# A gated cross-attention and mixture-of-experts block: row stacks built by selection matmuls, one list of steps, experts per sequence

## The reference, cut to what matters

```
x = x + tanh(g_xattn) * attention(layernorm(x), ctx)                 # 256 x 512 scores per sequence, one head
X = layernorm(x)
q, k, v = rmsnorm(X, n1) @ wq, @ wk, @ wv                            # 16 heads of 8 features
X = X + softmax(q k^T / sqrt(8)) v @ wo                              # 256 x 256 scores, 64 (sequence, head) pairs
h2 = rmsnorm(X, n2)
combine = top-2 of softmax(h2 @ router)                              # 8 experts
X = X + shared_expert(h2) + sum_e combine[e] * expert_e(h2)          # silu(h2 @ gate) * (h2 @ up) @ down, 256 hidden
x = x + tanh(g_ffn) * X
```

## Time and profile before

| | us |
|---|---|
| median of 3 runs | 249.63 (249.5 to 251.0) |
| the profiled execution's own time | 249.14 |
| its span in the profile | 247.4 |
| mean granted PE clock | 0.92 of full speed |
| DMA | 12.83 MB, 50 GB/s of HBM traffic over the span |

### The profile page before, as it was taken

One profiled execution on the slowest core, in us unless ns is written; L12 is line 12 of the kernel. 1 busy time (PEld: TensorE's weight loads), 2 busy tenths in 40 slices (PEclk: granted clock), 3 DMA queues, 4 the chain that ended last, 5 costly groups with the idle time before them and its releaser, 6 DMA issues.

```text
span 247.4 us, 3838 instructions
## 1 busy us (share of the span) xinstructions
PE 202.7 (82%) x1327; PEld 161.2 (65%) x1327; DVE 152.5 (62%) x393; ACT 101.3 (41%) x203; POOL 58.8 (24%) x77
## 2 busy tenths in 40 slices
PE   7699695659783798299888577899789999999994
PEld 5467464446572566167665455688668888888883
DVE  3779999647653175446687642478874654655653
ACT  8153265930162274246584565423231221221320
POOL 8566969310140020011011011003302332000000
PEclk9999998865679599869999999999979999999999
DMA  6900002535934023400000010000002230000002
GB/s 175 269 0 4 0 16 72 153 104 121 229 103 105 7 90 85 91 3 5 9 1 5 3 48 0 3 0 0 4 0 64 87 107 0 21 3 1 1 3 85
DMA packets 7124, 12.83 MB, mean 52 GB/s; under 512 B 992, under 2 KB 4576, under 8 KB 6592
## 3 DMA queue, kind: packets, MB, share of 16 engines
...
## 4 chain that ended last, share of the span: by engine, by line
PE 48%; DVE 19%; DMA 12%; SPq 11%; issue 3%; ACT 3%; POOL 2%; DVEq 0%; ACTq 0%; POOLq 0%
PE bank L1066 12%; PE bank L1083 7%; PE bank L1085 6%; PE bank L1084 6%; DMA split_scratch<-split 5%; DMA q_st<-negmT 5%; PE bank L1052 5%; SPq L320 4%; SPq L323 4%; PE bank L1037 4%; PE bank L1026 3%; DVE mxs L822 2%; DVE xs L696 1%; DVE small L703 1%; DVE y L690 1%
## 5 line engine op out<-in xcount | busy, mean ns | idle before, releaser
L822 DVE TENSOR_REDUCE mxs<-bank 128x2 f32<-128x512 f32 x64 | 42.5, 689 | 27.9 <-PE bank L1026 27.4
L588 ACT ACTIVATE ep<-bank 128x512 f32<-128x512 f32 x64 | 37.5, 595 | 35.3 <-PE bank L1037 34.7
L1037 PE MATMUL bank<-q_st,k_st 128*128 128x256 f32 x128 | 28.8, 311 | 16.7 <-DMA q_st<-negmT 13.3
L1026 PE MATMUL bank<-k_st,q_st 128*128 128x256 f32 x128 | 34.3, 363 | 2.2 <-DVE mxs L822 1.1
L1066 PEld LDWEIGHTS bank<-down_s,vx 128*128 128x128 f32 x288 | 34.9, 193 | 1.8 <-issue 0.4
L1066 PE MATMUL bank<-down_s,vx 128*128 128x128 f32 x288 | 35.2, 276 | 0.0
L612 ACT ACTIVATE silu<-bank 128x512 f32<-128x512 f32 x28 | 16.6, 598 | 43.9 <-PE bank L1085 43.9
L1037 PEld LDWEIGHTS bank<-q_st,k_st 128*128 128x128 f32 x128 | 21.9, 210 | 18.5 <-DMA q_st<-negmT 13.9
L1083 PE MATMUL bank<-h2hi,whi 128*128 128x512 f32 x72 | 30.8, 428 | 2.7 <-ACT silu L612 2.7
L1026 PEld LDWEIGHTS bank<-k_st,q_st 128*128 128x128 f32 x128 | 23.5, 231 | 10.5 <-issue 4.5
L1085 PE MATMUL bank<-h2hi,wlo 128*128 128x512 f32 x72 | 29.1, 404 | 0.0
(11 more groups left out here) (139 smaller groups left out, 288.4 us busy)
## 6 DMA issues: line engine op xcount, KB each, us to landing
...
```

The source lines that it names most:

```text
L588: nc.scalar.activation(ep[:, n % NEP].rearrange("p t s -> p (t s)"), b_of(("exp", n))[:], ACT.Exp, scale=SCALE_H).then_inc(free(("exp", n) ...
L822: nc.vector.tensor_reduce(mxs[:, n // NH, :, n % NH], b_of(("max", n))[:].rearrange("p (t s) -> p t s", t=TB), AX_X, ALU.max).then_inc(fre ...
L1026: last = pe.matmul(b_of(("max", n))[:, j * L:(j + 1) * L], q_st[:, b % NSTACK, h // 2, j * P:(j + 1) * P], k_st[:, b % NSTACK, k_slot(h), ...
L1037: last = pe.matmul(b_of(("exp", n))[:, j * L:(j + 1) * L], k_st[:, b % NSTACK, k_slot(h), j * P:(j + 1) * P], q_st[:, b % NSTACK, h // 2, ...
```

## The change

Five things are changed together.

1. The rows of `q_st` and `k_st` (now 96 rows, two of each) are made by PE: `make_stacks` multiplies 0/1 selection matrices (`sel_q`, `sel_k`, made by POOL from the identity) with the two parts of q and k. Sixteen steps "e" (four for each sequence), each 8 matmuls of 256 columns into two banks of the "proj" pair. ACT copies k's rows out (two copies of 32 x 512) and, from the second sequence on, q's rows (96 x 512); DVE copies q's rows of the first. The DRAM scratch and all its DMAs go.
2. The maxima of 8 heads stand in columns 64 to 79 of a 96-wide `mxs`, so that the transposes put them on rows 64 to 79; ACT writes them, negated, straight from PSUM into `q_st` (32 rows x 1024). `negmT` and its DMAs go.
3. One list of small steps (FIRST_STEPS, then MIXED_STEPS by a slot) takes the place of the x slots: the first a slot comes after four tiles of the cross-attention, and the other four tiles, the norms and steps e4 to e15 are set among a slots 0 to 47. LAG is 12.
4. An item is one expert on one sequence (256 tokens): 36 items with 12 matmuls of 256 columns, one silu of 128 x 512, one product, 8 down instructions. Item 0 begins at slot 47, item 1 at 62, and from slot 64 on one every second slot. Those begun up to slot 75 use tanh.
5. All nine experts' split weights stay in SBUF, so no load waits for an item. The output leaves in four parts.

```diff
-NSTACK = 3
-LAG = 13
+LAG = 12
 PV_LAG = LAG + 2
 
-M_STEPS = [("mT0", 8, 8), ("mT1", 17, 17)]
-C_STEPS = [("uT0", 31, 31), ("uT1", 32, 32), ("cT", 34, 34), ("wo", 36, 36), ("square", 37, 37), ("h2", 38, 38),
-           ("h2T", 41, 41), ("router", 43, 43)]
-ROUTE_STEPS = [("route_exp1", 43, 43), ("route_top", 45, 45), ("route_exp2", 45, 45), ("route_weights", 46, 46)]
-A_FROM = 10
-A_PER_X = 6
-M_FROM = 68
-M_EVERY = 2
-T_FROM = 80
-T_EVERY = 2
-NEARLY = 4
+NSTACK = 2
+M_STEPS = [("mT0", 8, 8), ("mT1", 16, 16)]
+C_STEPS = [("uT0", 30, 30), ("uT1", 31, 31), ("cT", 33, 33), ("wo", 35, 35), ("square", 36, 36), ("h2", 37, 37),
+           ("h2T", 40, 40), ("router", 42, 42)]
+ROUTE_STEPS = [("route_exp1", 42, 42), ("route_top", 44, 44), ("route_exp2", 44, 44), ("route_weights", 45, 45)]
+FIRST_STEPS = """f0 g0 xn0 f1 q0 g1 s0 xn1 s1 p0 q1 o0 p1 s2 o1 f2 s3 n0 p2 g2 h0 o2 xn2 p3 k0
+                 e0 q2 e1 o3 e2 w0 e3 n1""".split()
+MIXED_STEPS = {0: "s4 h1", 1: "f3", 2: "k1 s5", 3: "p4 g3", 4: "e4 xn3", 5: "o4 p5", 6: "e5 q3", 7: "o5 s6", 8: "e6 n2",
+               9: "p6 s7", 10: "e7 h2", 11: "o6", 12: "p7 k2", 13: "w1", 14: "o7", 16: "n3", 17: "e8", 19: "h3",
+               21: "e9 k3", 25: "e10", 29: "e11", 31: "w2", 33: "e12", 37: "e13", 41: "e14", 45: "e15", 47: "w3"}
+EARLY_AT = {47: 1, 62: 1}
+EARLY_FROM, EARLY_EVERY = 64, 2
...
-    items = [(e, h) for h in range(2) for e in range(NEARLY)] + [(e, h) for e in range(NEARLY, NEXP) for h in range(2)]
-    NI = len(items)
-    last_item_of = {e: max(n for n, it in enumerate(items) if it[0] == e) for e in range(NEXP)}
-    thirds = [(n, k) for n in range(NI) for k in range(3)] + [(NI, 2)]
...
+    dense = [(0, 0), (0, 1)] + [(e, b) for b in range(2) for e in range(1, NEXP)]
+    dense += [(e, b) for b in range(2, NB) for e in range(NEXP)]
+    ND = len(dense)
+    last_exp = NHEADS - 1 + LAG
+    order = [step_of(text) for text in FIRST_STEPS]
+    begun = 0
+    tanh_items = []
+    def item(n):
+        return [("up", n)] + ([("down", n - 1)] if n else [])
+    for i in range(SLOTS_A):
         order.append(("a", i))
-        due = M_FROM <= i < T_FROM and (i - M_FROM) % M_EVERY == 0 or i >= T_FROM and (i - T_FROM) % T_EVERY == 0
-        if due and early < 3 * NEARLY:
-            order.append(("m", early))
-            early += 1
-    order += [("m", i) for i in range(early, len(thirds))]
-    pair_uses = {"turn": [("xnT", 0)], "proj": [("fold", 0), ("v", 0), ("q", 0)], "sum": [], "misc": []}
+        order += [step_of(text) for text in MIXED_STEPS.get(i, "").split()]
+        if i in EARLY_AT or i >= EARLY_FROM and (i - EARLY_FROM) % EARLY_EVERY == 0:
+            order += item(begun)
+            if i <= last_exp:
+                tanh_items.append(begun)
+            begun += 1
+    for n in range(begun, ND):
+        order += item(n)
+    order.append(("down", ND - 1))
...
-        def stack(sp, b):
-            ...
...
-        def place_m(sp, b, half):
-            ...
...
+            for e in range(NEXP):
                 load_expert(sp, e)
+            for b in range(NB):
+                is_read(sp, ("down", max(n for n, it in enumerate(dense) if it[1] == b)))
+                sp.dma_start(out[:, TB * b:TB * (b + 1)], x1[:, TB * b:TB * (b + 1)]).then_inc(out_stored, 16)
+            sp.wait_ge(out_stored, 16 * NB)
...
+            def select_rows(part):
+                heads = ident[:].rearrange("p (g i d) -> p g i d", i=2, d=DH)
+                for i in range(2):
+                    one = heads[:, :, i].unsqueeze(2).broadcast_to([P, NG, 2, DH])
+                    rows_q = sel_q[:, part, :, 32 * i:32 * i + 32].rearrange("p g (a c d) -> p g a c d", a=2, c=2)
+                    nc.gpsimd.tensor_copy(rows_q[:, :, part], one).then_inc(sel_ready, 1)
+                    rows_k = sel_k[:, part, :, 32 * i:32 * i + 32].rearrange("p g (a c d) -> p g a c d", a=2, c=2)
+                    nc.gpsimd.tensor_copy(rows_k[:, :, :, part], one).then_inc(sel_ready, 1)
+            def clear_pads(s):
+                words = k_st[:, s].bitcast(F32)
+                step(nc.gpsimd.memset(words[0:32, NG:], 0.0))
+                nc.gpsimd.memset(words[32:64, :NG], 0.0).then_inc(pads_ready, 1)
+                pool.wait_ge(pads_ready, s + 1)
...
+            norm1(0)
+            norm1(1)
+            pool.wait_ge(ld_attn, 16)
+            pool.wait_ge(tg_ready, 1)
+            step(nc.gpsimd.tensor_scalar(bv_row, bv_row, tg[:, 0:1], None, ALU.mult))
             add_bias(0)
             add_bias(1)
+            for part in range(2):
+                select_rows(part)
+            norm2(0)
+            pool.wait_ge(norm2_out, 1)
+            clear_pads(0)
+            norm1(2)
+            nc.gpsimd.memset(mxs[:], 0.0).then_inc(mxs_ready, 1)
+            step(nc.gpsimd.memset(vh[:], 0.0))
+            nc.gpsimd.memset(vh[:, :, :, DH:DH + 1], 1.0).then_inc(vh_ready, 1)
+            add_bias(2)
+            norm2(1)
             norm1(3)
+            add_bias(3)
+            pool.wait_ge(xb_ready, 4)
+            clear_pads(1)
             pool.wait_ge(ld_ffn, 16)
             nc.gpsimd.tensor_copy(router_pad[:, 0:NE], router_s).then_inc(router_ready, 1)
             split_weights(0)
+            norm2(2)
             split_weights(1)
             norm2(3)
+            for e in range(2, 4):
                 split_weights(e)
+            norm3(0)
+            split_h2(0)
+            for e in range(4, 7):
+                split_weights(e)
+            norm3(1)
+            split_h2(1)
+            for e in range(7, NEXP):
+                split_weights(e)
+            for b in range(2, NB):
                 norm3(b)
                 split_h2(b)
...
+            def copy_picks(s):
+                picks = ident[64:NSEL, 64:64 + NH].rearrange("r (g p) -> r p g", p=2)
+                for p in range(2):
+                    nc.scalar.copy(k_st[64:NSEL, s, p * NG:(p + 1) * NG, :],
+                                   picks[:, p].unsqueeze(2).broadcast_to([32, NG, L])).then_inc(picks_ready, 1)
+            act.wait_ge(ident_ready, 1)
+            copy_picks(0)
...
+            def stacks_out(i):
+                b, part = i // 4, i % 4
+                s, gs = b % NSTACK, 2 * part
+                if b >= NSTACK:
+                    is_full(act, ("exp", NH * (b - NSTACK) + 4 * part + 3))
+                if i == 0:
+                    act.wait_ge(pads_ready, 1)
+                if i == 4:
+                    act.wait_ge(pads_ready, 2)
+                if b > 0:
+                    is_full(act, ("stq", i))
+                    nc.scalar.copy(q_st[0:NSEL, s, gs:gs + 2, :].rearrange("p g s -> p (g s)"),
+                                   b_of(("stq", i))[0:NSEL]).then_inc(free(("stq", i)), 1)
+                is_full(act, ("stk", i))
                 for p in range(2):
+                    last = nc.scalar.copy(k_st[32 * p:32 * p + 32, s, p * NG + gs:p * NG + gs + 2, :].rearrange("p g s -> p (g s)"),
+                                          b_of(("stk", i))[32 * p:32 * p + 32])
+                    if p == 0:
+                        last.then_inc(k_half, 1)
+                last.then_inc(free(("stk", i)), 1)
             def misc(step, b):
                 if step in ("mT0", "mT1"):
                     half = int(step[2])
+                    use = ("mT", b, half)
                     is_full(act, use)
+                    rows = b_of(use)[64:NSEL, 0:L].unsqueeze(1).broadcast_to([32, NG // 2, L])
+                    nc.scalar.mul(q_st[64:NSEL, b % NSTACK, 4 * half:4 * half + 4, :], rows, -1.0).then_inc(free(use), 1)
...
+            def dense_up(n):
+                is_full(act, ("gate", n))
                 if n >= 2:
+                    is_read(act, ("up", n - 2))
+                if n in tanh_items:
+                    nc.scalar.activation(silu[:, n % 2], b_of(("gate", n))[:], ACT.Tanh, scale=0.5).then_inc(tanh_ready, 1)
                 else:
+                    nc.scalar.activation(silu[:, n % 2], b_of(("gate", n))[:],
+                                         ACT.Silu).then_inc(free(("gate", n)), 1)
...
+                elif stage == "k":
+                    qk_split(i)
+                    if i == 0:
+                        copy_picks(1)
...
+            def stack_out(i):
+                use, gs = ("stq", i), 2 * i
+                is_full(dve, use)
+                nc.vector.tensor_copy(q_st[0:NSEL, 0, gs:gs + 2, :].rearrange("p g s -> p (g s)"),
+                                      b_of(use)[0:NSEL]).then_inc(free(use), 1)
...
+            def make_stacks(i):
+                b, part = i // 4, i % 4
+                if i == 0:
+                    pe.wait_ge(sel_ready, 8)
+                pe.wait_ge(hi_ready, b + 1)
+                written(("qk2", b))
+                for qk, use, rows in ((0, ("stq", i), sel_q), (1, ("stk", i), sel_k)):
+                    may_fill(pe, use)
+                    for n in range(2):
+                        for hl in range(2):
```

(30 more changed lines are left out.)

741 lines of the change are left out of this document (302 added, 439 removed).

## The result

The changed kernel took 265.45 us in the median of four runs (263.74 to 267.53), the kernel before 250.25 beside it: ratio 1.061, 95% interval 1.053 to 1.070. The prediction was 243.9 with a range to 260, so it was wrong in sign and in size.

What follows compares the result with a forecast made beforehand. It took PE to bound most of the span, with DVE fullest in the cross-attention and maxima DMA waits holding the third stretch. Six stage terms summed to 242.2 us, plus 1.7 around the span: 243.9, range 228 to 260.

Steps and rivals of the forecast that it cites:

- A: From 0 to the first product for a maximum: 43.0 us, bounds 40 to 47.
- B: Slots 0 to 11, with four cross-attention tiles: 26 us, bound by DVE, between 22 and 30.
- C: Slots 12 to 16: 6 us, from PE's 5.2 plus waits.
- D: Slots 17 to 47: 44.5 us, PE (sum 41) and ACT (sum 40) nearly full together, plus slack.
- E: Slots 48 to 63: 20 us, from 17.55 for 16 earlier slots and 2.3 for item 1.
- F: From slot 64 to the end: 102.7 us, with items of 2.33 us and a routing stall of 4.2.
- 5.7: Before the first maximum: us for three row-making steps, 2.0 each less a little overlap.
- Rival (2): Row-making steps and exponentials' products contend for "proj" banks, slots 4 to 45: 3.5 us a step, 262.6 total; chance 0.2.
- 1.085: Slots 17 to 47: slack factor from undisturbed slots, taking PE's sum of 41 to 44.5 us.
- (1) Full overlap: Whole kernel: everything overlaps, PE's sums without slack, 225.7 us; chance 0.15.
- (3) The clock: B and D: short PE waits lower its clock to a mean of 0.75, 8.8 us more, 252.7; chance 0.12.
- (4): Routing amid silu items: four table loads fully on the path, 5.1 us more, 249.0; chance 0.08.

Runs made afterwards that it cites:

- e15: Not a run: the last of the changed kernel's sixteen steps that make stack rows, four for each sequence; no time of its own was measured.
- e2: The changed kernel with the selection products of the row-making steps in banks "sum" and "misc" instead of "proj": 259.5 us, ratio 1.038 to the kernel before.
- e1: The changed kernel with POOL's clearing of the second stack's pads moved to right after the third bias addition: 260.6 us, ratio 1.043 to the kernel before.
- f1: The changed kernel without the row-making steps of sequences 2 and 3, which use the rows of 0 and 1: 255.35 us, ratio 1.020 to the kernel before.
- e8: Not a run: the changed kernel's first row-making step for sequence 2, with eight selection matmuls and three copies; no time of its own was measured.
- e3: The changed kernel with q's 12 copies, from the second sequence on, on DVE instead of ACT: 266.9 us, ratio 1.059 to the kernel before.
- e4: The changed kernel with tanh instead of silu for all items begun up to slot 92: 266.5 us, ratio 1.069 to the kernel before.
- f4: The kernel before with only the maxima changed, ACT writing them straight from PSUM into `q_st`: 232.6 us, ratio 0.929 to the kernel before.

## Why the prediction was wrong, by its own steps
The six pieces, predicted and measured (at the cuts of the windows above): A 43.0 and 46.45; B 26 and 32.07; C 6 and 11.18; D 44.5 and 49.50; E 20 and 23.13; F 102.7 and 101.5. The differences add up to 21.6 us, the whole miss of the span (242.2 against 263.8).

**A, 3.4 short, within its bounds of 40 to 47: "5.7" for steps e1 to e3.** The split ended at 32.57 (33.2 predicted), the copies of the picks at 35.57 (36.1) and the first copies of k's rows at 36.77 (37.3): every term up to there was good within 0.6. The rest took 9.7 us instead of 5.7. "A projection's copy between" was priced at its length. But the projection (L867) first waits 1.46 us for the copy that empties the step's bank, then takes 2.04 us, and the next step comes after it. The clock is in it too: it was 0.54 from 36.90 to 41.70, and the four matmuls for q of one step took 1.20 us at 38.61 and 0.71 at 41.71. e2 shows the size of the bank's part: with other banks the first maximum comes 6.0 us sooner (3.8 to 7.0 against all equal starts). Rival (2) had the mechanism and put it into the wrong stage.

**B, 6.1 short: "DVE bounds it".** DVE was busy for 20.41 us where I had 25.7, PE for 24.08 where I had 20, and neither bounded 32.07. The step that failed is the rule "the sum of its fullest engine": it needs an engine with a queue of work ahead of it, and in this stage a slot's product, a maximum, a norm and a step e alternate between four engines (in the chain of waits from 46 to 90 us no line has more than 8.9%). Of the 6.1 us, e1 accounts for 3.8, POOL's late clear. The prediction counted these memsets where they meet the first sequence's second norm (right: from POOL's power at 21.18 to the norm's end at 25.07 are 3.9 us, 3.5 counted), and not at all for the other stack. The norms within the slots meet POOL's work as well:

```profile
L652 DVE TENSOR_SCALAR y<-x,mv,small x8: 335/958/1495, 21.6 to 87.8; 128x128 f32<-128x128 f32 x8
```

The shortest, the median and the longest of the eight are 0.335, 0.958 and 1.495 us for the same tile. The two at 46.59 and 46.84, with POOL idle, took 0.335 and 0.339; the six beside a memset, a cast or a subtraction of POOL took 0.461 to 1.495. What else is in the 6.1 wasn't parted. PE's terms were nearly right: in f1, with a clock of 0.94 in these slots, it was busy for 20.9 us.

**C, 5.2 short: "PE's 5.2 plus waits".** PE was busy for 8.37 us and waited 2.8. Step e8, which the prediction counted in D, is in this window with its eight matmuls, and so are the products of a sixth slot and the transposes of the maxima. The waits were taken as 0.8. PE waited 1.02 for DVE's half of the split and 1.79 for the maximum of slot 15: its product was out by 84.3, but in DVE's queue the last tile's x1 and the first steps of the last norm (83.60 to 86.18) stood before it.

```profile
86.83 0.42 PE L942 MATMUL bank<-ident,mxs 128*96 128x128 f32 x2 [1.79 <-DVE mxs L782]
...
88.65 0.71 PE L930 MATMUL bank<-split,sel_q 128*96 128x256 f32 x4
```

**D, 5.0 short: the factor "1.085" and PE's sum.** The PE sum of 41 was measured as 43.3, ACT's of 40 as 38.95, and the parts of ACT's are good: the copies (0.582 and 0.575 for a predicted 0.585) and the maxima's write (1.016 for 1.02):

```profile
L513 ACT ACTIVATE q_st<-bank 32x1024 fp32r<-32x1024 f32 x8 | 8.1, 1016 | 1.9 <-PE bank L942 1.6
```

What failed first was the working. The row that gives the slack has 17.55 us for a sum of 15.5, which is 1.13 and not 1.085. With it D would have been 46.4 and the whole 245.8. Applied to the measured 43.3 the same 1.13 gives 49.0 (48.4 by the 15.71 us that PE was busy in that row), against 49.50. So the idea of a sum with the slack of undisturbed slots came near in this stage; 1.9 us of the miss are the slip and 2.6 the 2.3 that PE's sum lacked, though e8's matmuls are in C's window. (The rivals took D's PE sum as 39.5, where it is 41.) ACT was 79% busy here, between the 85 to 90 forecast and the 75 that was to show rival (2). Its price of 3.5 a step and its bank mechanism were wrong here (e2; f1 measured 1.25 a step), and nothing supports ACT's sum as a bound (e3).

**E, 3.1 short.** I took the earlier trace rows's undisturbed 17.55 us and item 1. In the row that I used there was no routing. Here the first pair's, on DVE from 150.96 to 158.53, falls into these slots, and the next maxima wait in DVE's queue: between those at 152.44 and at 156.41 there are fifteen steps, L713 to L727. The kernel before had its routing in the same slots (132.02 to 138.85) and took 19.1 us for them, 1.5 more than the row. The other part is the clock in item 1: after PE had waited 2.15 us for ACT's copy the granted clock was 0.60 (157.10 to 161.40), and the item's twelve matmuls took 2.71 us (157.73 to 160.44) instead of 1.44. The two come to 2.8 of the 3.1, if they add up; no run parts them.

```profile
157.13 0.95 PE L949 MATMUL bank<-ident,u 128*128 128x128 f32 x4 [2.15 <-ACT u L557]
```

**F, right within 2.** (From the end of the last maximum, where the forecast had its cut, it was 100.8.) An item is 2.307 us (15 of them from 221.94 to 256.54 in the chain; 2.33 predicted). The stall of the last routing was 3.29, of the 4.2 counted, and there are six table loads, as predicted, if the one at the very start is counted. The timeline of ACT around the routing:

```profile
203.88 0.60 ACT L568 ACTIVATE early<-bank 128x512 f32<-128x512 f32 x1 [0.23 <-PE bank L1041]
204.49 1.28 ACT L537 ACT_TABLE_LOAD   x1
206.77 0.23 ACT L537 ACTIVATE rt<-rt 128x32 f32<-128x32 f32 x1 [0.99 <-DVE rt L710]
207.01 1.28 ACT L568 ACT_TABLE_LOAD   x1
208.31 0.60 ACT L568 ACTIVATE early<-bank 128x512 f32<-128x512 f32 x1
208.93 1.28 ACT L540 ACT_TABLE_LOAD   x1
```

Each load is 1.28 us and begins within 0.02 us of the end of what stands before it. The Trainium skill (ScalarE: Activation LUTs, "What ACT_TABLE_LOAD costs") adds a drain of 1380 ns to each switch; the trace again shows none, and in e4, with four switches fewer, the last piece was 1.4 us shorter.

**The rivals.** (1) Full overlap: false, by 40 us. (2) Banks: true for 4 to 7 us at the start, false in the slots; that its 262.6 came within 3 us of the result is luck. (3) The clock: 0.84 in B, just below the 0.85 that it had as its sign, but 1.00 in C and D. (4) Not borne out: e4's last piece was 1.4 shorter where it had 5.1.

**The sign.** The prediction judged the change as one sum. D was added up from the new stage's parts, so the 13.3 us of DMA waits that go and the steps that come never stood apart, and it came out at 44.5 against 47.2. Set apart by f4, the relief was 16.6 us in slots 12 to 47, and all else added 7.6 + 16.3 in the same slots, 10.0 of it the steps e8 to e15 (f1). Part 2 needs nothing of parts 1, 3, 4 and 5 and could have been priced by itself.

Whose waits the 13.3 us are is less clear than their name. The wait list of the kernel before has, beside the row, only this one for the stacks' DMAs:

```profile
PE bank L1026 <- DMA k_st<-split_scratch: 0.9, 1, 0.9
```

But its chain goes through the stacks' DMAs and their issues before it comes to the placement of the maxima:

```profile
64.54 5.16 DMA split_scratch<-split
...
74.61 0.65 SPq L323
...
75.36 6.40 DMA q_st<-negmT
```

ACT had these maxima ready at 73.65; SP issued their DMA at 75.36, behind the stack's eight. By the times of their semaphores in the trace, the three placements that PE waited for (issued at 62.28, 75.36 and 98.99, each soon after the eight issues that read a stack back) landed 6.4 to 6.5 us after their issue, the other five 2.4 to 2.5. So part 1, which takes the stacks' DMAs away, might have removed the long waits without part 2. No run has part 1 alone, so it stays open whether the 16.6 us that part 2 gained needed part 2. f4 does show that, with the placements gone, the stacks' DMAs cost PE no wait in the slots. Their price is then ahead of the first product, where the changed kernel did gain.
